# The value gathers of a graph layer as a loop on the engine, with the index columns copied into two small tiles

## The reference, cut to what matters

```python
xn = layernorm(x)
x = x + gnn(xn, src, dst) + mix(xn)          # mix: linear attention with feature maps
x = x + ffn(layernorm(x))                     # ffn: 8 experts, Sinkhorn gates, top-k routing

# inside gnn
e = leaky_relu(el[src] + er[dst])             # 8 heads
exp_e = exp(e - segment_max(e, dst)[dst])
a = exp_e / segment_sum(exp_e, dst)[dst]
rst = segment_sum(feat_v[src] * a, dst)       # feat_v: 6250 x 512, 8 heads of 64
```

## Time and profile before

| | |
|---|---|
| median of 3 runs | 3646.91 us (3639.39 to 3655.47) |
| the profiled execution's own time | 3658.21 us |
| its span, from the first to the last instruction | 3656.2 us |
| mean granted TensorE clock | 0.904 |
| PE busy | 2752.1 us, 75% |
| POOL busy | 2339.4 us, 64% |
| DVE busy | 1545.9 us, 42% |
| ACT busy | 986.0 us, 27% |
| DMA packets | 337,888, 382.27 MB |

### The profile page before, as it was taken

One profiled execution on the slowest core, in us unless ns is written; L12 is line 12 of the kernel. 1 busy time (PEld: TensorE's weight loads), 2 busy tenths in 40 slices (PEclk: granted clock), 3 DMA queues, 4 the chain that ended last, 5 costly groups with the idle time before them and its releaser, 6 DMA issues.

```text
span 3656.2 us, 48084 instructions
## 1 busy us (share of the span) xinstructions
PE 2752.1 (75%) x10604; PEld 1745.2 (48%) x10605; DVE 1545.9 (42%) x2472; ACT 986.0 (27%) x2524; POOL 2339.4 (64%) x1895
## 2 busy tenths in 40 slices
PE   1557999999999888821077788898989999711499
PEld 1555667766776554511043444455555555410244
DVE  3441222222222277711943444555555556563132
ACT  0111222222222100002034444455555555400011
POOL 5455777777777777765078887787777777303422
PEclk9999999999999999965599999898899999855799
DMA  7542222222222233341055656666777777601332
GB/s 182 133 138 45 48 43 38 51 40 43 45 40 51 57 95 90 88 70 14 7 147 159 163 161 166 176 176 173 179 181 184 179 184 187 192 0 27 81 85 66
DMA packets 337888, 382.27 MB, mean 105 GB/s; under 512 B 192332, under 2 KB 222214, under 8 KB 337465
## 3 DMA queue, kind: packets, MB, share of 16 engines
q0 software_dynamic: 227264, 228.52, 28.0%
q1 hardware_dynamic: 110578, 153.26, 14.6%
HBM read 288.24 MB, written 80.92 MB: 101 GB/s over the span
## 4 chain that ended last, share of the span: by engine, by line
POOL 35%; PE 19%; issue 19%; DMA 10%; DVE 10%; DVEq 3%; SPq 2%; ACT 1%; ACTq 0%; POOLq 0%
POOL R L542 27%; PE ps L602 17%; DMA R<-val_tab,src_i 7%; POOL R L561 6%; DMA work<-in_x_dram 3%; POOL er_starts L529 1%; DVE R L1238 1%; DVEq L1241 1%; DVE sm L1323 1%; PE ps L621 1%; DVEq L1238 1%; PE ps L826 1%; DVE R L1274 1%; DVE work L1277 1%; DVE R L1272 1%
## 5 line engine op out<-in xcount | busy, mean ns | idle before, releaser
L602 PE MATMUL ps<-R,work 125*125 (+4 forms) x5640 | 1878.8, 482 | 121.0 <-DVE R L1238 103.1
L602 PEld LDWEIGHTS ps<-R,work 125*125 125x125 f32 (+2 forms) x5640 | 965.7, 204 | 958.2 <-issue 954.1
L561 POOL DMA_INDIRECT R<-val_tab,src_i x800 | 1042.9, 1304 | 396.5 <-issue 180.5
L542 POOL DMA_INDIRECT R<-el_tab,src_i x800 | 986.8, 1234 | 334.5 <-issue 334.5
L1238 DVE TENSOR_TENSOR R<-R (+1 forms) x800 | 507.0, 688 | 587.2 <-POOLq L567 430.7
L942 ACT ACTIVATE work<-work 125x125 f32<-125x125 f32 x900 | 277.6, 308 | 531.1 <-PE ps L602 516.9
L939 ACT ACTIVATE work<-work,negdst 125x125 f32<-125x125 f32 x900 | 353.2, 392 | 137.2 <-issue 123.3
L602 PE MATMUL ps<-work,R 128*128 128x250 f32 x1600 | 358.6, 383 | 14.4 <-DMA work<-R 14.4
L602 PEld LDWEIGHTS ps<-work,R 128*128 128x128 f32 x1600 | 308.4, 194 | 51.4 <-issue 14.5
L582 POOL DMA_INDIRECT xs_tab<-R,slot_s x50 | 59.6, 1192 | 218.2 <-issue 218.2
L1115 DVE TENSOR_TENSOR R<-ps,R 125x512 f32<-125x512 f32 x50 | 34.6, 692 | 370.7 <-PE ps L602 370.7
(11 more groups left out here) (209 smaller groups left out, 2236.6 us busy)
## 6 DMA issues: line engine op xcount, KB each, us to landing
work<-in_x_dram SPq DMA_DIRECT2D x100, 250.0 KB
R<-el_tab,src_i POOLq DMA_INDIRECT x800, 3.1
R<-val_tab,src_i POOLq DMA_INDIRECT x800, 5.8
R<-xs_tab SPq DMA_DIRECT2D x56, 225.8 KB, 2.6
xs_tab<-R SPq DMA_DIRECT2D x50, 252.0 KB
R<-work SPq DMA_DIRECT2D x25, 500.0 KB, 4.9
work<-R SPq DMA_DIRECT2D x25, 500.0 KB, 8.9
val_tab<-R SPq DMA_DIRECT2D x50, 250.0 KB
```

The costliest lines, as they stand in the source:

```text
L542: eng.indirect_dma_start(out=ELP[:, t % CT, t // CT, :], out_offset=None, in_=el_tab[:, :], in_offset=bass.IndirectOffsetOnAxis(ap=src_i[: ...
L561: eng.indirect_dma_start(out=ring[:, (2 * u + s) % RING, :], out_offset=None, in_=val_tab[:, :], in_offset=bass.IndirectOffsetOnAxis(ap=sr ...
L602: return pe.matmul(o, l, r, start=start, stop=stop)
```

## The change

The Python loop over 400 pairs on POOL becomes a trip of 16 pairs (32 tiles) that is written out once ahead, once in a loop on the engine of 23 turns, and once behind: 25 trips. In a loop the index column of a gather must have a fixed place, so the columns are first copied, 16 at a time, from `src_i` into one of two small tiles `idx[0]`, `idx[1]` (125 x 16 integers each, in `work`), by a plain DMA transfer that POOL issues (`load_idx`). One copy is made ahead of all trips, and each trip makes two, but the last only one: 50 copies. The gather reads its column from there. Each half of a trip begins with a wait for its copy. The wait for room in the ring now stands before a raise of `pool_passed`, with a number that comes from the loop's counter, and so does the wait in `report`.

```diff
+        idx = [wk(3700 + RING * k, RING)[0:P, :].bitcast(INT32) for k in range(2)]
...
+        idx_in = [sem(f"idx_in{k}") for k in range(2)]
...
-            def gather_pair(u):
+            def load_idx(i, k):
+                eng.dma_start(idx[k], src_i[:, bass.ds((2 * i + k) * RING, RING)]).then_inc(idx_in[k], 16)
+
+            def gather_pair(q):
                 for s in range(2):
-                    eng.indirect_dma_start(out=ring[:, (2 * u + s) % RING, :], out_offset=None, in_=val_tab[:, :],
-                                           in_offset=bass.IndirectOffsetOnAxis(ap=src_i[:, 2 * u + s:2 * u + s + 1], axis=0))\
-                        .then_inc(gathered[u % PAIRS], 16)
-
-            def report(u):
-                eng.wait_ge(gathered[u % PAIRS], 32 * (u // PAIRS + 1))
+                    n = 2 * q + s
+                    eng.indirect_dma_start(out=ring[:, n % RING, :], out_offset=None, in_=val_tab[:, :],
+                                           in_offset=bass.IndirectOffsetOnAxis(ap=idx[n // RING][:, n % RING:n % RING + 1], axis=0))\
+                        .then_inc(gathered[q % PAIRS], 16)
+
+            def report(i, q):
+                if q < 0:
+                    i, q = i - 1, q + 2 * PAIRS
+                eng.wait_ge(gathered[q % PAIRS], 32 * (2 * i + q // PAIRS + 1))
                 eng.sem_inc(S["vals_ready"], 2)
 
-            for u in range(ET // 2):
-                if u == 2:
-                    eng.wait_ge(S["weights_kept"], NB)
-                eng.wait_ge(S["tile_free"], 2 * u + 2)
-                gather_pair(u)
-                if u >= BEHIND:
-                    report(u - BEHIND)
-            for u in range(ET // 2 - BEHIND, ET // 2):
-                report(u)
+            def trip(i, last=False):
+                for q in range(2 * PAIRS):
+                    u = 2 * PAIRS * i + q
+                    if q % PAIRS == 0:
+                        eng.wait_ge(idx_in[q // PAIRS], 16 * (i + 1))
+                    if isinstance(u, int) and u == 2:
+                        eng.wait_ge(S["weights_kept"], NB)
+                    eng.wait_ge(S["tile_free"], 2 * u + 2)
+                    eng.sem_inc(S["pool_passed"], 1)
+                    gather_pair(q)
+                    if not isinstance(u, int) or u >= BEHIND:
+                        report(i, q - BEHIND)
+
+                    if q == BEHIND:
+                        load_idx(i, 1)
+                    if q == PAIRS + BEHIND and not last:
+                        load_idx(i + 1, 0)
+
+            NTRIP = ET // (2 * RING)
+            load_idx(0, 0)
+            trip(0)
+            with eng.Fori(1, NTRIP - 1) as i:
+                trip(i)
+            trip(NTRIP - 1, True)
+            for q in range(2 * PAIRS - BEHIND, 2 * PAIRS):
+                report(NTRIP - 1, q)
```

## The result

The changed kernel takes 3685.66 us (median of 4 runs, 3677.8 to 3693.81) against 3643.15 us of the kernel before (4 runs, 3629.33 to 3655.47). The ratio is 1.0118, 95% interval 1.0073 to 1.0163: slower by some 42 us, where 27 were forecast (3674 us). The profiled execution took 3681.73 us, its span 3679.8 us, 23.6 us more than before.

The account below looks back on a forecast made before the run. POOL was taken to pace the message stage, with 33 us of slack; copies +43 us less 16 us of slack gave +27 us on the 3646.9 us median, 3674 us, range 3638 to 3708 (forecast's own 3657 to 3690).

Parts of the forecast that it names:

- POOL sets the pace of the message stage: Message stage: POOL has only 33 us of true slack in 1311, so further GpSimd work comes nearly in full on top.
- The price of a copy: Index copies on POOL: 0.58 us plus a 0.30 us gap each, 43 us for 49; bounds 27 and 74 us.
- Half of the slack is taken: Message stage: copies use half of POOL's 33 us of free time, taking 16 us off their 43.
- The sum: Whole kernel: +43 - 16 = +27 us, 3674 us for the median; chance 0.55.
- The waits for the copies: POOL's waits ahead of each half trip: copies have normally landed by then, so they cost nothing.
- the sequencer's work: Register waits, raise and branch on POOL: some 0.5 us a pair, hidden beside three queued gathers; cost nothing, uncovered 199 us.
- the room in the ring: Wait for `tile_free` moved ahead of the gather: counted as nothing, perhaps 0.1 to 0.2 us later where PE is late.
- Collisions with DVE: Gathers lengthened by DVE multiplications, 76 us of the stage: change taken as zero, open from -76 to +99 us.
- The rival of a phase in favour: Message stage: later reports put DVE's multiplications behind gather starts, removing two thirds of 76 us, 3623 us; chance 0.09.
- The loop's turn stalls the sequencer: POOL's 23 loop turns each fetch instructions, 1.3 us each, 30 us in all, 3704 us; chance 0.12, shared with dear copies.
- The copies vanish in the slack: Message stage: copies of 0.56 us without gap mostly fit POOL's free time, +8 us, 3655 us; chance 0.19.
- The verdict: Measured class of the whole kernel: slower by over 0.5% 0.62, within 0.28, faster 0.10.

Follow-up runs that it names:

- written out: Changed kernel with all 25 trips written out, no loop on the engine, 50 copies kept: 3671.99 us, ratio 1.0075 to the kernel before.
- The loop's stage: Changed kernel with each index tile copied only once, ahead of all trips, run twice: 3659.97 and 3658.61 us, ratios 1.0033 and 1.0028 to the kernel before.

## Why the prediction was right, and where it was off

*POOL sets the pace of the message stage.* Held. 55 us of added GpSimd work lengthened the stage by about 40.

*The price of a copy.* 0.58 + 0.30 us was forecast, 0.60 measured. The duration was right. The gap was not: it stands ahead of a gather, and a plain transfer behind a gather has none. The lower bound, 0.56, was the nearer. The term is 29.4 us, not 43.

*Half of the slack is taken.* 16 us were forecast. Against the 34.1 us of before, the three profiles with 49 copies give 13.0 (slack 21.1), none (37.8) and 7.6 us (26.5). So half was too much, and the size of the term isn't settled by three executions.

*The sum.* With the right price and the forecast's half of the slack it would have been 29 - 16 = 13 us. The stage grew by 18.5, 25.6 and 30.0 us in the three profiles and the medians by 42. The copy was priced 14 us too high and the slack taken too large by 3 to 16 us; the two errors went opposite ways, and that 27 lies among the three stages is in part luck. The runs put the copies at 20 us (written out) to 33 us (in the loop). What is left of the 42 us, some 0.3%, comes with the edited kernels on the first chip but is no larger than the ratio of an unedited one; its cause is open, and the prediction has no term for it.

*The waits for the copies, the sequencer's work, the room in the ring.* Held: in the message stage no gather waited for a copy, the instructions of a turn took 135 ns, the raise 17 ns in the median, and the gaps stayed at 0.30 us. The sequencer's added work in the stage sums up to some 33 us, 0.08 for a pair, where up to 0.5 was forecast; by program order three gathers were queued at 224 of 397 reports, and at 231 before. The loop's stage was 1307.8 and 1310.0 us, against 1311.0.

*Collisions with DVE.* Taken as zero, between -76 and +99 us. Measured: +2.1 and -7.3 us in the sum of the gathers in the two profiles of the changed kernel; 1295 to 1310 ns in the mean in twelve of the fourteen profiles and never beyond 1294 to 1315. The rival of a phase in favour is out.

*The loop's turn stalls the sequencer.* Out. Instruction queues moved 6 packets in 1200 us and none in the 840 us with 15 of the 23 turns, and no gap marked issue was longer than 0.8 us. So these turns, each of a trip of 32 tiles, show no fetch and no stall. That a fetch would take as long as a gather's landing, 5.8 us, was the author's assumption, and no run shows it.

*The copies vanish in the slack.* Out: 1.0118, 1.0120 and, written out, 1.0075 have intervals above 1, and the stages with 49 copies, 1329.5 to 1341.0 us, were all longer than those without copies on the first chip, 1307.8 to 1323.0.

*The verdict.* Slower by over 0.5% had a chance of 0.62. The time, 3685.66 us, lies in the stated range of 3638 to 3708, and inside the forecast's own range of 3657 to 3690.

## What to carry to other kernels

POOL, which prepares the transfers here, was busy or in its gaps of 0.30 us for all but some 34 of 1311 us, and of 55 us of further transfers some three quarters came on top of the stage. A copy cost it 0.60 us with 64 bytes in each row and with 320, so 9 copies of 80 columns took 5 us of the engine where 49 of 16 columns took 29. Look at what a loop needs beside the loop (here copies, since the author took a loop to need index columns at fixed addresses; no run tried a column that follows the counter) and make that rare. And where a kernel's executions spread by 1% for reasons ahead of the edit, compare the edited stage in several profiles, and run the kernel against itself once before believing 0.3%.

## What the runs showed of the hardware that was not expected

- The gap of 0.30 us ahead of an indirect transfer on POOL isn't there ahead of a plain one: a plain copy of 125 rows of 64 bytes took 0.60 us back to back with a gather, and three in a row took 0.59 us for the first and 1.11 for the two others. Behind a memset of 0.47 us the gather's gap was 0.18.
- A plain transfer took 599 ns with 64 bytes in each row and with 320. Begun inside a DVE multiplication it took 599 ns too (18 of 50), where gathers begun inside one took 1464 ns in the mean (305 of 800) and the others 1209.
- The stage ahead of the edit has two lengths, about 15 us apart, with the gap ahead of the 742nd gather at 2.4 to 9.9 us or at 15.3 to 20.0, by whether it began more than a microsecond after SyncE's 16 transfers.
- A loop of 16 pairs on GpSimd's sequencer turned in 135 ns of instructions, and in the 840 us with 15 of its turns no instruction packet moved.
